# Second attention: GpSimd halves the state products of 12 of 16 heads, VectorE sums the other four heads in an instruction of its own

## What is computed

```python
retention = jnp.einsum('bhsd,bhtd->bhst', q, k) * SCALING
retention = retention * decay[None]              # causal, gamma_h ** (s - t)
out = jnp.einsum('bhst,bhtd->bhsd', retention, v)
out = (out - mean) * jax.lax.rsqrt(var + EPS)    # per head, over its 8 channels
gate = jax.nn.silu(x @ Wg.T)
return gate * out @ Wo.T
```

## Time and profile before

| | us |
|---|---|
| median of 3 runs | 1167.25 (1165.15 to 1167.34) |
| the profiled execution, its own time | 1176.8 |
| its span, first to last instruction | 1175.0 |

### The profile page before, as it was taken

How to read it: one execution, slowest core, us unless ns; L and a number is a source line. 1 busy time by engine, 2 the same in 40 slices (tenths; PEclk the granted TensorE clock), 3 DMA queues, 4 the chain that set the end, 5 groups by cost and what they waited for, 6 DMA issues and landing times. The chain is left out here.

```text
span 1175.0 us, 25297 instructions
## 1 busy us (share of the span) xinstructions
PE 950.1 (81%) x5489; PEld 689.5 (59%) x5489; DVE 901.3 (77%) x2728; ACT 640.5 (55%) x1626; POOL 790.2 (67%) x656
## 2 busy tenths in 40 slices
PE   3799999999778688888988953788858687989884
PEld 2565555555446455555555532556648587888773
DVE  2589999999949769888888966486656595777765
ACT  1555555444279556676677533676528205756652
POOL 0288888888712179999999957678706204777776
PEclk9899999999979889999999985799955557989997
DMA  7320000000000220000000005234423103333331
GB/s 217 102 88 1 0 0 0 0 0 0 1 1 0 81 64 18 9 18 18 9 18 18 10 27 153 67 95 105 106 69 103 50 1 91 99 99 102 102 100 45
DMA packets 67118, 61.25 MB, mean 52 GB/s; under 512 B 7812, under 2 KB 54096, under 8 KB 67042
## 3 DMA queue, kind: packets, MB, share of 16 engines
q1 hardware_dynamic: 58978, 41.47, 12.7%
q0 software_dynamic: 6912, 18.36, 5.4%
q10 hardware_dynamic: 1152, 0.52, 0.2%
HBM read 30.97 MB, written 21.50 MB: 45 GB/s over the span
## 5 line engine op out<-in xcount | busy, mean ns | idle before, releaser
L462 PE MATMUL a_pS<-a_kv,utri 128*128 128x360 f32 (+3 forms) x768 | 264.8, 481 | 19.4 <-issue 6.5
L453 POOL TENSOR_TENSOR a_kv<-a_qk,a_vv 128x1152 f32<-128x1152 f32 (+1 forms) x128 | 264.1, 2064 | 13.2 <-DVE a_qk L427 13.2
L558 POOL TENSOR_TENSOR a_tt<-a_tt 128x576 f32<-128x576 f32 (+1 forms) x128 | 157.0, 1227 | 64.1 <-DVE a_tt L542 64.0
L462 PEld LDWEIGHTS a_pS<-a_kv,utri 128*128 128x128 f32 x768 | 136.3, 191 | 100.6 <-DVE a_tt L542 30.5
L542 DVE TENSOR_TENSOR a_tt<-a_pS,a_qk 128x360 f32<-128x360 f32 (+3 forms) x384 | 180.8, 525 | 15.5 <-PE a_pS L462 8.5
L1761 POOL DMA_INDIRECT x_yl<-ys,e_row x72 | 70.5, 979 | 80.5 <-POOLq L1472 54.2
L570 DVE TENSOR_REDUCE a_nd<-a_tt 128x144 f32<-128x720 f32 (+3 forms) x128 | 104.2, 814 | 0.0
L508 ACT ACTIVATE a_tt<-a_pI 128x144 f32<-128x144 f32 (+1 forms) x96 | 40.1, 417 | 111.7 <-PE a_pI L470 111.7
L1707 PE MATMUL x_pZ<-w,x_hT 128*128 x576 | 82.0, 287 | 12.1 <-issue 8.9
L501 PEld LDWEIGHTS a_pO<-wgate,a_yT 128*128 128x128 f32 x256 | 42.8, 194 | 81.1 <-issue 51.8
L1767 POOL DMA_INDIRECT out_dram<-x_o,e_row_z x72 | 74.2, 1031 | 22.5 <-issue 21.1
(11 more groups left out here) (260 smaller groups left out, 2445.1 us busy)
## 6 DMA issues: line engine op xcount, KB each, us to landing
ys<-gw SPq DMA_DIRECT2D x16, 256.0 KB, 3.7
xs<-X SPq DMA_DIRECT2D x16, 256.0 KB, 2.3
X<-xs SPq DMA_DIRECT2D x16, 256.0 KB, 5.5
m_kx<-m_kc SPq DMA_DIRECT2D x64, 64.0 KB, 2.0
ys<-X SPq DMA_DIRECT2D x16, 256.0 KB, 2.9
m_ax<-m_pc SPq DMA_DIRECT2D x64, 64.0 KB, 2.0
ys<-U SPq DMA_DIRECT2D x16, 256.0 KB
w<-in_L_ffn_W_dram SPq DMA_DIRECT2D x1, 2048.0 KB
```

What stands on the lines that cost most here:

```text
L453: pool.tensor_tensor(kv[:, t % 2, :, :, :], kk.unsqueeze(2).to_broadcast([P, H, J, D]), vv[:, t, :, :].unsqueeze(3).to_broadcast([P, H, J, ...
L462: pe.matmul(pS[c][:, 0:(h1 - h0) * SC], K.utri[:, :], flat[:, h0 * SC:h1 * SC], start=True, stop=True).then_inc(u_done, 1)
L558: pool.tensor_tensor(tt[:, t % 2, :, :, D // 2:D], tt[:, t % 2, :, :, D // 2:D], tt[:, t % 2, :, :, 0:D // 2], ALU.add).then_inc(half_done, 1)
```

## The change

In the second attention GpSimd's halving covers heads 0 to 11 only. VectorE reduces heads 12 to 15 over all eight products (and the ninth place for t > 0) in an instruction of its own, ahead of its wait for the halving, and then the other twelve heads as before. In layer 0 the constant `HALVED` is 16, so that nothing is left out of the halving and the extra instruction isn't issued; there only the place of the wait in the list of waits ahead of the sum is another.

```diff
+    HALVED = H if layer == 0 else 12
...
             pool.wait_ge(t_done, 3 * n + 3)
-            pool.tensor_tensor(tt[:, t % 2, :, :, D // 2:D], tt[:, t % 2, :, :, D // 2:D],
-                               tt[:, t % 2, :, :, 0:D // 2], ALU.add).then_inc(half_done, 1)
+            pool.tensor_tensor(tt[:, t % 2, 0:HALVED, :, D // 2:D], tt[:, t % 2, 0:HALVED, :, D // 2:D],
+                               tt[:, t % 2, 0:HALVED, :, 0:D // 2], ALU.add).then_inc(half_done, 1)
...
             n = 4 * b + t
-            v.wait_ge(half_done, n + 1)
             v.wait_ge(t_done, 3 * n + 3)
             rows = D
             if t > 0:
                 v.wait_ge(inter_ready, 3 * b + t)
                 rows = D + 1
             wait(v, y_ready, n - 1)
-            v.tensor_reduce(nd[:, t % 2, :, :], tt[:, t % 2, :, :, D // 2:rows], AX.X, ALU.add).then_inc(red_done, 1)
+            if HALVED < H:
+                v.tensor_reduce(nd[:, t % 2, HALVED:, :], tt[:, t % 2, HALVED:, :, 0:rows], AX.X, ALU.add)
+            v.wait_ge(half_done, n + 1)
+            v.tensor_reduce(nd[:, t % 2, 0:HALVED, :], tt[:, t % 2, 0:HALVED, :, D // 2:rows], AX.X, ALU.add)\
+             .then_inc(red_done, 1)
```

## The result

The changed kernel takes 1177.87 us (median of 4 runs, 1175.41 to 1179.88) against 1167.3 (1165.15 to 1168.36). The ratio is 1.0092, 95% interval [1.0066, 1.0118]: slower, by 7.7 to 13.8 us. The forecast was 1175.2, in a range of 1171 to 1180. A second comparison, on a chip where the kernel before takes 1230.5 us, gave 1.0058 [1.004, 1.0076]. The 8.0 us of the forecast are 1.0068, inside both. The median came out 2.7 us above the forecast, so the traces have to say how much of the difference is the change's.

What follows compares the result with a forecast made beforehand. VectorE's chain, with its waits for ScalarE's square root, was taken to bound the second attention, not GpSimd. Fifteen batches at +0.47 us (7.0) plus 1.0 for the last gave +8.0, scaled to 7.9: 1167.25 to 1175.2 us, range 1171 to 1180.

Steps and rivals of the forecast that it cites:

- The pacer: Second attention: VectorE's chain and waits set the steps, not GpSimd, though GpSimd is busy 16.57 of 17.36 us a batch.
- The price of the sum: VectorE's sum in two instructions costs +0.197 us a tile: 0.133 for 128 more elements, 0.064 for the extra instruction.
- steps t = 0 and t = 2: First and third tile of a batch: VectorE works without a gap to the variance sum, so each grows by 0.197 us.
- Rival D: Each VectorE instruction pays its full duration, 0.277 us extra a sum: 13.2 us in all, 1180.4 us; chance 5%.
- Step t = 1: Second tile of a batch, where GpSimd's gain lands: with the first tile 8.14 us instead of 8.07, +0.07.
- Step t = 3: Fourth tile of a batch: the sum delays ScalarE's squares, so +0.197 us despite VectorE's 1.22 us wait.
- rival C: ScalarE's squares in the fourth tile wait for something else, so it costs nothing: 5.1 us in all, 1172.3 us; chance 12%.
- The moved wait: VectorE's wait for GpSimd's halving, now between the two reductions: met 2.6 us earlier, so costed at nothing.
- The sum: Total over the second attention: 7.0 us for fifteen batches plus 1.0 us for the last, +8.0 us.
- A: GpSimd is the pacer: the batch falls by 0.70 us, 10.5 us in 15 batches, to 1156.8 us; chance 6%.
- B: VectorE's idle time and earlier yT from GpSimd absorb everything: within 0.2%, about 1168 us; chance 5%.
- E: The second tile has no slack, so all 64 sums pay in full: 12.6 us, 1179.9 us; chance 7%.

Runs made afterwards that it cites:

- relief_only: Kernel before, with GpSimd halving 12 heads instead of 16 in layer 1 and VectorE's sum unchanged; ratio 0.9972, batch 17.14 us.
- longer_sum_only: Kernel before, with VectorE's two reductions as in the changed kernel and GpSimd still halving all 16 heads; ratio 1.0087, batch 17.94 us.
- split_only: Kernel before, with VectorE's layer 1 sum split in two instructions over the same products, GpSimd still halving 16 heads; ratio 1.0034, batch 17.60 us.
- root_first16: Kernel before, with ScalarE's square root ahead of the norm's weights in every tile of layer 1; ratio 0.996, batch 16.89 us.
- root_odd16: Kernel before, with ScalarE's square root ahead of the norm's weights in the second and fourth tiles only, layer 1; ratio 0.9937, batch 16.74 us.
- after_again: The changed kernel run again without edit, against the kernel before; ratio 1.0058, batch 17.82 us.

## Why the prediction was right

- **The pacer.** The step that decided was to follow the starts of VectorE's products instead of the busy shares. relief_only and longer_sum_only measured the two halves apart: -3.3 and, without the longer branch and the one long step, +7.6. Together they aren't a sum: the 3.3 vanish once VectorE's chain is longer than GpSimd's in t = 1. That is the 8.14 against 7.84 of the prediction.
- **The price of the sum.** 0.197 from the two sizes of the old sum and its start-to-start distance. The reductions took 443 and 644 ns in the mean, 442 and 642 were worked out, and the steps t = 0 and t = 2 grew by 0.20. Rival D, the full durations, is out by split_only's 0.06. The prediction took only half of what the Trainium skill says on the drain ("VectorE: DVE Perf Modes", "The DRAIN you can't avoid"): the same section adds that a next operation that isn't held starts earlier. The trace agrees: the second reduction started 0.09 us before the first had ended (565.21 against 564.85 + 0.45). So rival D is not what the Trainium skill says of this pair.
- **Step t = 1.** Forecast +0.07 for t = 0 and 1 together, measured 8.13 against 8.07. VectorE's own chain for t = 1 with the old sum, worked out as 3.81, stands alone in root_first16 and root_odd16: 3.80.
- **Step t = 3.** The thin point was whether the squares or L399 bind. The idle time of 0.28 us in front of the squares settles it, and rival C is out: 5.55, not 5.36. The margin was thin: the sum moved by 0.20, and the idle time before it had been 0.07. In root_first16, where ScalarE comes 0.34 us later, the squares start 0.17 us behind the sum's end (568.35) and 0.15 behind the start of the copy L399 (568.37), so there the copy binds and no longer the sum.
- **The moved wait** cost nothing, as costed.
- **The sum.** +8.0 forecast, +7.6 and +7.7 in the traces. Into and in the last batch the steps grew by 0.19 to 0.20 as said, from 5.03, 3.74, 3.59 and 3.73; a batch grew by 0.45 instead of 0.47, and the first batch by less, since its first tile has no sum. That is the 0.4 us between. The median's +10.6 is further off, and that 1177.87 lies so near 1175.2 rests in part on the scatter of the runs.
- **Wrong in detail:** GpSimd's idle time isn't 0.3 in every tile but 1.65, 0.20, none and 0.20. Most of it lies in t = 0, where the wait was already.
- **Rivals A, B and E.** A's gain isn't there in relief_only (17.14, not 16.66). B is out by the time and by the steps: t = 0, t = 2 and t = 3 grew by 0.19 to 0.20 each, and nothing was paid back. E (no slack in t = 1) would have shown 3.94 + 4.13 + 0.39 = 8.46 for the first two steps.

## What to carry to other kernels

An engine that is busy 95% of a stage need not be its bound; follow the starts of one instruction from iteration to iteration and ask which wait ends last in each step. Moving work from a full engine to a less full one costs at the receiver's place in the chain: here VectorE had 1.6 us of idle time a batch and was given 0.79 us of sums, and the batch grew by 0.45. The wait of 0.37 us in t = 1, which GpSimd set, took in 0.33 of them. The wait of 1.22 us in t = 3 took in none, because the sum stood ahead of the operation on ScalarE that ended it. A reordering that shortens one step must be followed through the step before it as well, as root_first16 shows.

## What the runs showed that I had not expected

**The loop's branch has two lengths.** On VectorE the same loop shows 0.29 us of idle time at its branch in all kernels but two, and 0.41 in split_only and longer_sum_only, whose bodies have one reduction more, as after has. Where the loop is entered (batch 1) these two show 0.37 us of idle time as well, and the others none; here before and longer_sum_only:

```profile
438.02 1.36 DVE L542 TENSOR_TENSOR a_tt<-a_pS,a_qk 128x384 f32<-128x384 f32 x3
```
```profile
435.74 1.35 DVE L542 TENSOR_TENSOR a_tt<-a_pS,a_qk 128x384 f32<-128x384 f32 x3 [0.37 <-issue]
```

With 13 branches back and one entry that is 13 x 0.12 + 0.36 = 1.9 us. Taken off, split_only's stretch grew by 2.0 us (2.2 expected). What decides the form wasn't tried and stays open.

**TensorE's clock at the start of the attention.** In some executions it is up and in others not, whatever the kernel (1.00 is 2.4 GHz, and a mean between 0.5 and 1 mixes this level with 1.2 GHz). The changed kernel twice (first the profile of the result, then after_again; PE and PEld, the clock is the third column from the end):

```profile
412.00:420.00 8.00, 4.96 (x13) 2.91 (x12) 2.20 (x7) 5.13 (x10) 5.95 (x5) 0.71 0.77 225
```
```profile
412.00:420.00 8.00, 4.95 (x22) 3.26 (x21) 3.26 (x11) 4.74 (x10) 6.92 (x6) 1.00 0.59 176
```

With a mean of 0.71 of full speed the first products start 17.06 us after the clearing of the values and the second tile 5.00 later; at 1.00 it is 15.69 and 3.18. That is 3.2 us between two executions of one program, 40% of the effect under study.
